# Layer-0 outputs of a two-layer kernel: head pairs one after another instead of in couples, each pair's scores on two row strips, layer norm from partial statistics

## The reference, cut to what matters

```python
x = x + s * g                       # s: attention output of layer 0 (projected) plus its input, g: gate
xn = _layernorm(x, axis=-1)         # (x - mean) / sqrt(var + 1e-5)
q, k, v = split(xn @ W_attn)        # 16 heads of 8
q_l, k_l = landmarks(q), landmarks(k)                    # means of 16 tokens: 64 landmarks
N = softmax(einsum('bhld,bhtd->bhlt', q_l, k), axis=-1)  # 64 x 1024 for each head
K = softmax(einsum('bhld,bhmd->bhlm', q_l, k_l))         # 64 x 64
NV = N @ v
```

## Time and profile before

| | us |
|---|---|
| median of 3 runs | 1328.98 (1327.92 to 1329.9) |
| profiled execution | 1327.18 |
| its span | 1325.1 |
| mean granted TensorE clock | 0.962 |
| PE busy in the span | 1204.9 (91%) |
| DVE busy | 999.6 (75%) |
| ACT busy | 837.6 (63%) |
| POOL busy | 260.2 (20%) |

### The profile page before, as it was taken

One profiled execution on the slowest core, in us unless ns is written; L12 is line 12 of the kernel. 1 busy time (PEld: TensorE's weight loads), 2 busy tenths in 40 slices (PEclk: granted clock), 3 DMA queues, 4 the chain that ended last, 5 costly groups with the idle time before them and its releaser, 6 DMA issues. The chain is left out here.

```text
span 1325.1 us, 32172 instructions
## 1 busy us (share of the span) xinstructions
PE 1204.9 (91%) x13377; PEld 607.5 (46%) x13377; DVE 999.6 (75%) x1256; ACT 837.6 (63%) x1447; POOL 260.2 (20%) x373
## 2 busy tenths in 40 slices
PE   6977999999999999999999978888899799899980
PEld 4641333333323232233323345555799566688870
DVE  5879999999999999999999546765775788433324
ACT  3643888888888888888888845565222466533331
POOL 4200220000101001000010011100573222145560
PEclk9986999999999999999999989998998899999995
DMA  4764123232233322323311112000010211223317
GB/s 144 204 203 98 28 67 75 46 78 66 58 81 82 69 66 57 81 54 65 80 43 73 74 54 61 23 17 17 18 45 28 71 37 36 60 79 102 103 41 193
DMA packets 75229, 95.36 MB, mean 72 GB/s; under 512 B 13236, under 2 KB 44684, under 8 KB 74052
## 3 DMA queue, kind: packets, MB, share of 16 engines
q1 hardware_dynamic: 69996, 83.19, 24.4%
q0 software_dynamic: 5088, 10.12, 2.5%
HBM read 54.30 MB, written 38.56 MB: 70 GB/s over the span
## 5 line engine op out<-in xcount | busy, mean ns | idle before, releaser
L614 DVE TENSOR_REDUCE b_mx<-psum 128x2 f32<-128x1024 f32 x507 | 596.0, 1219 | 36.7 <-PE psum L558 27.9
L668 ACT ACTIVATE b_exp_ring<-psum 128x512 f32<-128x512 f32 x1024 | 540.0, 598 | 121.6 <-PE psum L725 120.8
L725 PE MATMUL psum<-b_q,b_k 75*32 75x512 bf16 x4096 | 315.4, 384 | 1.3 <-ACT b_exp_ring L668 1.1
L699 PE MATMUL psum<-b_exp_ring,b_v 128*32 128x512 f32 x2048 | 266.3, 595 | 0.7 <-ACT b_exp_ring L668 0.7
L557 PE MATMUL psum<-b_k,b_q 64*128 64x512 bf16 x512 | 188.4, 396 | 21.8 <-DVE b_mx L614 12.2
L558 PE MATMUL psum<-b_ko,b_qo 64*128 64x512 bf16 x512 | 188.4, 396 | 0.0
L725 PEld LDWEIGHTS psum<-b_q,b_k 75*32 75x32 bf16 x4096 | 86.5, 95 | 173.6 <-ACT b_exp_ring L668 112.3
L557 PEld LDWEIGHTS psum<-b_k,b_q 64*128 64x128 bf16 x512 | 47.3, 93 | 229.8 <-issue 132.7
L744 POOL CAST b_top<-b_mt 16x128 bf16<-16x128 f32 x32 | 8.9, 279 | 574.5 <-DVE b_mt L622 574.5
L1839 ACT ACTIVATE e_hT<-psum,e_b 128x358 f32<-128x358 f32 (+3 forms) x96 | 53.6, 559 | 75.4 <-PE psum L1859 72.0
L699 PEld LDWEIGHTS psum<-b_exp_ring,b_v 128*32 128x32 f32 x2048 | 60.8, 111 | 55.7 <-issue 9.6
(11 more groups left out here) (279 smaller groups left out, 1457.2 us busy)
## 6 DMA issues: line engine op xcount, KB each, us to landing
b_q<-q_ops SPq DMA_DIRECT2D x48, 192.0 KB
b_k<-k_ops SPq DMA_DIRECT2D x48, 192.0 KB
k_ops<-a_k SPq DMA_DIRECT2D x20, 256.0 KB, 3.4
x_disp<-b_zeros SPq DMA_DIRECT2D x13, 320.0 KB
e_x<-x_disp SPq DMA_DIRECT2D x8, 520.0 KB
v_ops<-a_vs SPq DMA_DIRECT2D x4, 1024.0 KB, 5.1
b_v<-v_ops SPq DMA_DIRECT2D x16, 256.0 KB
av_out<-b_acc SPq DMA_DIRECT2D x128, 32.0 KB, 1.7
```

Source lines behind the costliest of these rows:

```text
L614: nc.vector.reduce_max(mx[:, d % 2, :, i // 2, i % 2], pair, AX.X).then_inc(sem("b_max_done"), 1)
L668: act.activation(ex[:, n % E_RING, :], g.bank(5 + n % 3), ACT.Exp, scale=ATT_SCALE)\
L699: last = nc.tensor.matmul(AV[32 * i:32 * i + 32, :], v[s][:, at_v:at_v + 32], ex[:, (4 * group + i) % E_RING, :], start=(kb == 0), stop=(k ...
L725: last = nc.tensor.matmul(g.bank(5 + n % 3)[keys, :], k[s][0:XROWS, h, kb * P + 32 * j:kb * P + 32 * j + 32], q[s][0:XROWS, h, half * BANK ...
```

## The change

It touches only `layer0_outputs`. Pairs go in the order 0, 2, 4, 6, 1, 3, 5, 7, one after another, the k-th on D1 or D2 by turns. Scores of pair k + 2 wait only for the exponential of pair k, and PE's list is transposes k, scores k + 2, transposes k + 1, and so on. The first two pairs' scores are issued as a couple as before. From the third on, the first half of the tokens is computed on the pair's own strip from `qlm` and `kT`, the second half on the next strip from copies shifted by 32 partitions, `qlm_next` and `kT_next`, which SP fills by four DMAs per batch, ahead of its other work of that batch. The filler `busy` goes. The norm is cut into eight parts, one behind each maximum from the second on (the last two both behind the last maximum), and takes mean and variance from `bn_stats` and `bn_aggr` on tiles of 128 columns; part 5 is empty. The reciprocal of batch 0 moves to right behind the first maximum. In the last batch the router's pieces stand behind every second maximum. POOL clears four more semaphores at the start of the stage.

```diff
--- before.py
+++ after.py
...
-COUPLES = ((0, 2), (1, 3), (4, 6), (5, 7))
-NC = len(COUPLES)
+ORDER = (0, 2, 4, 6, 1, 3, 5, 7)
 VL = D + E
...
...
         oT = sb("c_oT", [P, T])
-        sm = sb("c_small", [P, 8, TB])
+        sm = sb("c_small", [P, 5, TB])
+        st = sb("c_stats", [P, TB, 6])
+        mv = sb("c_mean_var", [P, TB, 2])
         t1 = sb("c_t1", [P, TB, D])
-        xc = sb("c_xc", [P, TB, D])
         xT = sb("c_xT", [P, T])
...
         kT = sb("c_kT", [P, T])
+        kT_next = sb("c_kT_next", [P, T])
         vl = sb("c_vl", [P, TB, VL])
...
         qlm = sb("c_qlm", [P, HQ, LM])
+        qlm_next = sb("c_qlm_next", [P, HQ, LM])
         kx = sb("c_kx", [P, HQ, 2, LM])
...
...
     D0, D3, D1, D2 = (g.bank(2 * i, 2) for i in range(4))
-    s8, mu8, ss8, v8, rstd8, kmx, ksum, krec = (sm[:, i, :] for i in range(8))
+    v8, rstd8, kmx, ksum, krec = (sm[:, i, :] for i in range(5))
     tiles = lambda ap: ap.rearrange("p (n c) -> p n c", c=P)
...
...
     landmarks = lambda p: qlm[strip(p), 2 * (p % 2):2 * (p % 2) + 2, :].rearrange("p h n -> p (h n)")
-    place = lambda p: next(2 * c + pair.index(p) for c, pair in enumerate(COUPLES) if p in pair)
+    next_strip = lambda p: slice(32 * ((p // 2 + 1) % 4), 32 * ((p // 2 + 1) % 4) + 32)
+    next_landmarks = lambda p: qlm_next[next_strip(p), 2 * (p % 2):2 * (p % 2) + 2, :].rearrange("p h n -> p (h n)")
     mine = lambda n: slice(n * TB, (n + 1) * TB)
...
...
                     nc.vector.tensor_tensor(t1[:, :, :], tiles(D3), g.XN[:, mine(n), :], ALU.add).then_inc(sem("c_t1"), 1)
+                if part == 1:
                     dve.wait_ge(sem("c_t1"), done)
                     front(nc.vector.tensor_tensor(t1[:, :, :], t1[:, :, :], g.G[:, mine(n), :], ALU.mult))
-                if part == 1:
+                if part == 2:
                     front(nc.vector.tensor_tensor(g.X[:, mine(n), :], g.X[:, mine(n), :], t1[:, :, :], ALU.add))
-                    front(nc.vector.reduce_sum(s8, g.X[:, mine(n), :], AX.X))
-                    front(nc.vector.tensor_scalar(mu8, s8, 1.0 / D, None, ALU.mult))
-                if part == 2:
-                    front(nc.vector.tensor_tensor(xc[:, :, :], g.X[:, mine(n), :], over_last(mu8, D), ALU.subtract))
-                    front(nc.vector.tensor_tensor(t1[:, :, :], xc[:, :, :], xc[:, :, :], ALU.mult))
                 if part == 3:
-                    front(nc.vector.reduce_sum(ss8, t1[:, :, :], AX.X))
-                    nc.vector.tensor_scalar(v8, ss8, 1.0 / D, EPS, ALU.mult, ALU.add).then_inc(sem("c_var"), 1)
-                    dve.wait_ge(sem("c_rstd"), done)
-                    nc.vector.tensor_tensor(g.XN[:, mine(n), :], xc[:, :, :], over_last(rstd8, D), ALU.mult)\
-                      .then_inc(sem("c_xn"), 1)
+                    for t in range(TB):
+                        nc.vector.bn_stats(st[:, t, :], g.X[:, n * TB + t, :]).then_inc(sem("c_stats"), 1)
+                if part == 4:
+                    dve.wait_ge(sem("c_stats"), 2 * TB * done - TB)
+                    for t in range(TB):
+                        nc.vector.bn_aggr(mv[:, t, :], st[:, t, :]).then_inc(sem("c_stats"), 1)
+                    dve.wait_ge(sem("c_stats"), 2 * TB * done)
+                    nc.vector.tensor_scalar(v8, mv[:, :, 1], EPS, None, ALU.add).then_inc(sem("c_var"), 1)
+                if part in (6, 7):
+                    if part == 6:
+                        dve.wait_ge(sem("c_rstd"), done)
+                    for t in range(TB // 2 * (part - 6), TB // 2 * (part - 5)):
+                        nc.vector.tensor_scalar(g.XN[:, n * TB + t, :], g.X[:, n * TB + t, :], mv[:, t, 0:1],
+                                                rstd8[:, t:t + 1], ALU.subtract, ALU.mult).then_inc(sem("c_xn"), 1)
...
...
-                for c in range(NC):
-                    for s in range(2):
-                        p = COUPLES[c][s]
-                        dve.wait_ge(sem("c_n_ps"), PAIRS * b + 2 * c + s + 1)
-                        nc.vector.reduce_max(nm[:, p:p + 1], (D1, D2)[s], AX.X, negate=True).then_inc(sem("c_nm"), 1)
+                for k in range(PAIRS):
+                    p = ORDER[k]
+                    dve.wait_ge(sem("c_n_ps"), PAIRS * b + k + 1)
+                    nc.vector.reduce_max(nm[:, p:p + 1], (D1, D2)[k % 2], AX.X, negate=True).then_inc(sem("c_nm"), 1)
                     if b + 1 < B:
-                        norm(b + 1, c)
-                    else:
-                        for part in ((0,), (1, 2), (3, 4), (5,))[c]:
+                        if k:
+                            norm(b + 1, k - 1)
+                        if k == PAIRS - 1:
+                            norm(b + 1, k)
+                    elif k % 2:
+                        for part in ((0,), (1, 2), (3, 4), (5,))[k // 2]:
                             router(part)
-                    if b == 0 and c == 0:
+                    if b == 0 and k == 0:
                         dve.wait_ge(sem("c_dens"), 16)
...
...
             g.clear(pool, "a_")
+            for name in ("d_oT", "d_t1", "d_var", "d_biased"):
+                g.clear(pool, name)
             outputs_of(EARLY)
...
...
-                def transposed_out(c, s):
-                    k = PAIRS * b + 2 * c + s
-                    p = COUPLES[c][s]
-                    act.wait_ge(sem("c_enT_ps"), k + 1)
-                    act.activation(enT[:, :, p * P:(p + 1) * P], tiles((D0, D3)[s]), ACT.Copy).then_inc(sem("c_enT"), 1)
-
-                for c in range(NC):
-                    for s in range(2):
-                        k, p = PAIRS * b + 2 * c + s, COUPLES[c][s]
-                        act.wait_ge(sem("c_nm"), k + 1)
-                        if c >= 1:
-                            act.wait_ge(sem("c_enT_ps"), k - 1)
-                        act.activation(en[:, s, :], (D1, D2)[s], ACT.Exp, bias=nm[:, p:p + 1],
-                                       accum_out=nden[:, p:p + 1]).then_inc(sem("c_en"), 1)
-                    if c >= 1:
-                        transposed_out(c - 1, 1)
-                    transposed_out(c, 0)
-                    if c == 0 and b == B - 1:
+                def transposed_out(k):
+                    p = ORDER[k]
+                    act.wait_ge(sem("c_enT_ps"), PAIRS * b + k + 1)
+                    act.activation(enT[:, :, p * P:(p + 1) * P], tiles((D0, D3)[k % 2]), ACT.Copy).then_inc(sem("c_enT"), 1)
+
+                for k in range(PAIRS):
+                    p = ORDER[k]
+                    act.wait_ge(sem("c_nm"), PAIRS * b + k + 1)
+                    if k >= 2:
+                        act.wait_ge(sem("c_enT_ps"), PAIRS * b + k - 1)
+                    act.activation(en[:, k % 2, :], (D1, D2)[k % 2], ACT.Exp, bias=nm[:, p:p + 1],
+                                   accum_out=nden[:, p:p + 1]).then_inc(sem("c_en"), 1)
+                    if k:
+                        transposed_out(k - 1)
+                    if k == 2 and b == B - 1:
                         act.wait_ge(sem("r_gx"), 1)
                         act.activation(g.gates[:, :, :], g.gx[:, :, :], ACT.Exp).then_inc(sem("r_exp"), 1)
-                transposed_out(NC - 1, 1)
+                transposed_out(PAIRS - 1)
                 act.wait_ge(sem("c_kx"), b + 1)
...
...
                 if b >= EARLY:
-                    pe.wait_ge(sem("c_xn"), b - EARLY + 1)
+                    pe.wait_ge(sem("c_xn"), TB * (b - EARLY + 1))
                 if b >= 1:
...
...
-                def n_scores(c):
-                    if c:
-                        pe.wait_ge(sem("c_en"), PAIRS * b + 2 * c)
+                def first_scores():
                     for half in range(2):
...
                         for s in range(2):
-                            p = COUPLES[c][s]
+                            p = ORDER[s]
                             last = nc.tensor.matmul((D1, D2)[s][:, keys], landmarks(p), kT[strip(p), keys],
...
-                def busy(columns):
-
-                    lo = 0
-                    while lo < columns:
-                        n = min(BANK, columns - lo)
-                        nc.tensor.matmul(D0[:, 0:n], g.wqkv1[:, 0:P], xT[:, 0:n], start=True, stop=True)
-                        lo += n
-
-                def transposed(c, s):
-                    k = PAIRS * b + 2 * c + s
-                    if c:
-                        pe.wait_ge(sem("c_enT"), k - 1)
-                        if s == 0:
-                            busy(3 * BANK // 2)
-                    pe.wait_ge(sem("c_en"), k + 1)
-                    if c == 0:
+                def n_scores(k):
+
+                    p, S = ORDER[k], (D1, D2)[k % 2]
+                    pe.wait_ge(sem("c_en"), PAIRS * b + k - 1)
+                    if k == 2:
+                        pe.wait_ge(sem("c_next"), 16 * 4 * (b + 1))
+                    nc.tensor.matmul(S[:, 0:BANK], landmarks(p), kT[strip(p), 0:BANK], start=True, stop=True)
```

(33 more changed lines are left out.)

## The result

The changed kernel takes 1337.6 us (median of 8 runs, 1331.74 to 1340.2) against 1329.33 for the kernel before (8 runs, 1327.92 to 1330.03): ratio 1.0055, 95% interval 1.0042 to 1.0067. It is slower, and it scatters over 8.5 us where the kernel before scatters over 2. I had forecast 1321.3, faster. The profiled execution took 1337.51 us with a span of 1335.4 (before 1327.18 and 1325.1).

What follows compares the result with a forecast made beforehand. A latency loop across PE, DVE and ACT, none full, was taken as the bound. Batch savings 2.3 + 0.5 + 2.35 + 2.5 = 7.7 us take 1328.98 to 1321.3 us; range 1317.5 to 1329.

Steps and rivals of the forecast that it cites:

- Prices of the loop: Start-to-start times between transposes, scores, maximum and exponential: 4.67 us for two pairs; DVE 2.39 a pair, bound by a hair.
- The one-round price of scores: Scores of a single pair, split over two strips on PE, take one round of 0.84 to 0.86 us.
- Rival (b): In the loop, a pair's score halves do not overlap: two rounds, 5.53 us per loop, 1329 in all; chance 0.06.
- Strips and the drain: PE changes between full rows and strips six times a batch: 0.2 us a visit, already in the price.
- Shifted copies, tail, queue order: SP's copy DMAs land in time, the norm's end and POOL's power fit, waiting loads do not matter: all cost nothing.
- POOL against DVE: POOL's multiply holds DVE's two-input norm pass: 1.9 us lost in batch 1, 0.6 in batch 0.
- The filler removed: The unread filler product in PE's idle time can go at no cost; its only use could be the clock.
- with the clock back about 7 us later, as now: In batch 3 the low clock ends after about 7 us; products with v at 24.2, 2.5 us saved.
- rival (a): Without the filler TensorE's clock falls in idles: 1328.8 with three episodes, chance 0.07; 1338.8 with seven more, chance 0.12.

Runs made afterwards that it cites:

- the one-strip kernel: Changed kernel with POOL's multiply held, loop filler and batch 3 filler, each pair's second half of scores put on its own strip: 1338.97 us, ratio 1.0112.
- 32-row fillers: Changed kernel with POOL's multiply held and loop filler products on 32 of the array's 128 rows: 1327.92 us, ratio 0.9986.
- the late product alone: Changed kernel with POOL's multiply held until the norm's last two-input pass, no filler: 1330.43 us, ratio 1.0004.
- the kernel before with the gap filler: Kernel before, its own filler kept, plus 1024 filler columns ahead of batch 3's first transposes: 1327.66 us, ratio 0.9983.

## Why the prediction was wrong

- *Prices of the loop* (0.93, 1.23, 1.26, 1.25; DVE 2.39 a pair): right within 0.12 us over six pairs. The one-round price of scores, taken from the half-speed row, holds. Rival (b)'s price doesn't: it has 5.53 us for two pairs, and the one-strip kernel took 3.41 a pair, of which 0.43 is filler. Batches 0 to 2 at full clock came to 21.80 to 21.85, forecast 21.61; batch 3 to 23.1, where the forecast had 24.2 with a slow stretch in it.
- *Strips and the drain*: no extra cost beyond the 0.2 us in the price, since the loop came out as priced.
- *Shifted copies, tail, queue order*: nothing, as said. Landing 2.5 us against 2.6 taken.
- *POOL against DVE*: the collision came in batch 1 as described, 3.34 us for one pass, which ended at +9.20. The earlier trace rows give 5.22 + 2.35 + 1.1 = 8.67 for that end; the text took 8.9 to 9.1 and names no row for the rest. POOL's product began at +5.76 and not at 5.2, only 0.10 us ahead of the pass, so that it went this way and not the other, cheaper one was luck. In batch 0 I took 0.6 between 0 and 1.3; it was 0. By the Trainium skill (SBUF — State Buffer, "Who interferes with whom") such a pass with one SBUF input does not contend with GpSimd, and the measurement, 1.63 us for the eight, agrees.
- *The step that failed*: "The filler removed: no reader, and it lay in PE's idle time", together with "with the clock back about 7 us later, as now" in batch 3. The filler was what brought the clock back: batch 3 was at the low clock for 31 us without it, not 7, and for 10 to 14 us with it put back. I weighed it as rival (a) and gave it 0.12 for the slower case; that its 1338.8 is near the measured 1337.6 is luck. Two things made that too little. The evidence against it, 6.46 of 10 us busy at a clock of 1.00 in another stage, was a stretch into which the clock had come high (it was still 0.52 in 1030 to 1040, with PE busy 8.46 of 10), and it has other products; it says nothing of whether a clock once lost returns. And its price, 2.5 us an episode of 7 us, took the length of an episode from a kernel that had the filler: without it they lasted 20 and 31 us. Two such episodes and one short one did what I had reckoned needed seven.
- *A link that was missing*: I let the stall behind POOL cost its own 1.9 us and never asked what PE does meanwhile. It idles 2.39 us, like the 2.55 of batch 3, which stood in the earlier trace rows right before the half-speed scores. A stall of one engine that leaves PE idle has two prices, its own and that of the clock.

Not tried: the norm's change by itself, and whether the low stretches before 775 us or in the later stages can be mended in the same way.

## What to carry to other kernels

Before taking out work of TensorE that nobody reads, look in the trace for what the clock does after the longest idle that remains, and take the filler out of the old kernel alone as the first experiment: here that single run (+21 us) told more than the whole schedule. Fill the gaps rather than the loop: one filler of 1.7 us where 2.5 us stood empty saved 6.6 us here, and 2.5 us in the kernel before, whose loop brought the clock back sooner. And place POOL's two-input products beside maxima or statistics of VectorE, not beside its two-input passes.

## What the runs showed that I had not expected

- PE's busy share can be 100% while the clock stays at 1.2 GHz for 30 us (18.00 of 18, and 29.95 of 30 with 32-row fillers); with full-row fillers it ended in 10 to 14 us.
- A filler at the low clock costs its double time and lengthens the path it should shorten: batch 3 went from 30.8 to 29.2 only, though the low stretch went from 31 to 14 us.
- A DVE pass with two SBUF inputs that starts 0.1 us behind POOL's product takes 3.34 us; eight statistics with one input, begun while POOL's product runs, take 1.63, nothing extra.
- Within the changed kernel the scatter follows the clock: its fastest run (1331.74) had a mean granted clock of 0.947, its slowest (1340.2) 0.937. Across kernels it doesn't: the late product alone scatters over 3.5 us with a low stretch of 31 us in its trace, the kernel before with the gap filler over 5.7 us with none.
- An idle of about 2.5 us was followed by the low clock every time, one of 1.6 to 1.95 us every second time.
